# Scores of a local-attention layer: one head per matmul on 64 rows by 32 columns of the array, instead of two heads zero-padded to 128 rows

## The reference, cut to what matters

```python
for i in range(DEPTH):                     # 6
    x = attn_layer(shift_tokens(x), Wqkv[i], q_scale[i], k_scale[i], Wo[i]) + x
    x = ffn_layer(shift_tokens(x), ln_g[i], ln_b[i], W1[i], b1[i], W2[i], b2[i]) + x

# attn_layer
q, k = l2norm(q) * qs, l2norm(k) * ksc     # per head, then rotary with cos, sin, scale
# local_attention: bq has 32 queries of a window, bk2 the 64 keys of this and the window before
sim = jnp.einsum('bhwie,bhwje->bhwij', bq, bk2) * QK_SCALE
sim = jnp.where(mask, -jnp.finfo(sim.dtype).max, sim)
attn = jax.nn.softmax(sim, -1)
out = jnp.einsum('bhwij,bhwje->bhwie', attn, bv2)
```

## Time and profile before

| | us |
|---|---|
| median of 3 runs | 2127.57 (2124.98 to 2128.31) |
| profiled execution, its own time | 2129.41 |
| span of the profiled execution | 2127.6 |
| PE busy | 1861.1 (87%) |
| DVE busy | 1542.8 (73%) |
| ACT busy | 1382.8 (65%) |
| POOL busy | 1261.5 (59%) |
| local layers, first to last scores | 525.3 to 2042.3 |
| mean granted clock of PE | 0.951 |

### The profile page before, as it was taken

One profiled execution on the slowest core, in us unless ns is written; L12 is line 12 of the kernel. 1 busy time (PEld: TensorE's weight loads), 2 busy tenths in 40 slices (PEclk: granted clock), 3 DMA queues, 4 the chain that ended last, 5 costly groups with the idle time before them and its releaser, 6 DMA issues. The chain is left out here.

```text
span 2127.6 us, 47771 instructions
## 1 busy us (share of the span) xinstructions
PE 1861.1 (87%) x18048; PEld 1032.7 (49%) x18048; DVE 1542.8 (73%) x2543; ACT 1382.8 (65%) x2862; POOL 1261.5 (59%) x1111
## 2 busy tenths in 40 slices
PE   3787787865799999999999999999999999999984
PEld 2333333343455555555555555555555555555541
DVE  2667666623687888878788878888878888878753
ACT  1243343432778777778777777877787877787751
POOL 3303030003787777777787777787777787777731
PEclk9698988977899999999999999999999999999996
DMA  7000000022433234233433225333343322323300
GB/s 159 1 2 1 2 1 1 1 60 49 101 77 74 66 81 89 72 75 75 83 80 78 68 67 98 71 80 71 72 85 76 85 66 69 76 66 79 83 21 20
DMA packets 142987, 131.78 MB, mean 62 GB/s; under 512 B 85160, under 2 KB 88808, under 8 KB 142440
## 3 DMA queue, kind: packets, MB, share of 16 engines
q1 hardware_dynamic: 142768, 128.83, 27.1%
HBM read 20.94 MB, written 1.05 MB: 10 GB/s over the span
## 5 line engine op out<-in xcount | busy, mean ns | idle before, releaser
L970 ACT ACTIVATE prob<-s_in,lower,rq 128x64 f32<-128x64 f32 x1536 | 537.9, 430 | 80.6 <-POOL lower L1079 78.5
L831 PE MATMUL bank_a<-x_shift,wqk_sb 128*128 128x512 f32 x768 | 374.6, 611 | 77.0 <-ACT sq L1000 57.9
L850 PE MATMUL bank_y<-zT,wvo 128*128 128x512 f32 x768 | 345.7, 593 | 0.0
L1059 POOL TENSOR_TENSOR sumk<-sq 128x512 f32<-128x512 f32 x96 | 122.5, 1276 | 278.2 <-ACT sq L1000 278.2
L831 PEld LDWEIGHTS bank_a<-x_shift,wqk_sb 128*128 128x128 f32 x768 | 140.1, 193 | 269.5 <-issue 148.2
L850 PEld LDWEIGHTS bank_y<-zT,wvo 128*128 128x128 f32 x768 | 146.1, 190 | 184.2 <-issue 184.2
L863 PEld LDWEIGHTS bank_z<-kpad,qpair 128*32 128x32 f32 x6144 | 164.6, 110 | 101.0 <-issue 98.9
L461 DVE TENSOR_REDUCE a_negmax<-a_max 128x1 f32<-128x512 f32 x256 | 164.6, 684 | 60.7 <-PE a_max L176 60.1
L863 PE MATMUL bank_z<-kpad,qpair 128*32 128x128 f32 x6144 | 187.6, 274 | 23.9 <-ACT zT L966 22.0
L377 ACT ACTIVATE a_prob<-a_sT 128x1024 f32<-128x1024 f32 x128 | 128.8, 1023 | 119.4 <-PE a_sT L208 118.2
L438 POOL TENSOR_TENSOR a_rstd<-a_mv,eps 128x4 f32<-128x4 f32 x4 | 0.8, 200 | 330.1 <-DVE a_mv L517 330.1
(11 more groups left out here) (161 smaller groups left out, 3944.7 us busy)
## 6 DMA issues: line engine op xcount, KB each, us to landing
qpair<-qfin SPq DMA_DIRECT2D x384, 128.0 KB, 2.4
kpad<-kfin SPq DMA_DIRECT2D x768, 64.0 KB, 2.0
wqk_sb<-in_wqkv SPq DMA_DIRECT2D x24, 256.0 KB, 5.6
xk_prev<-xk_own SPq DMA_DIRECT2D x24, 192.0 KB, 2.4
ffn_sb<-in_ffn SPq DMA_DIRECT2D x6, 537.5 KB, 3.9
wv_in<-in_wqkv SPq DMA_DIRECT2D x12, 256.0 KB, 4.9
wo_in<-in_wo SPq DMA_DIRECT2D x6, 512.0 KB, 6.3
xk_prev<-xk_own SPq DMA_DIRECT2D x24, 48.0 KB, 2.3
```

The lines of the kernel that those rows point to most:

```text
L831: last = pe.matmul(bank_a[:, half, :], wqk_sb[:, layer_of(u) % 2, part, half, g * P:(g + 1) * P], cols(u), start=True, stop=True)
L850: last = pe.matmul(bank_y[:].rearrange("p (t w q) -> p t w q", w=WPT, q=WIN), wvo[:, layer_of(u), GH * g + hh, :], zT[:, n % 2, :, :, hh, ...
L970: last = act.activation(prob[:, n % 2, i, :], s_in[:, n % 2, i, :], ACT.Exp, bias=lower[:, n % 2, i:i + 1], scale=rq[:, n % 2, i:i + 1])
L1059: pool.tensor_tensor(sumk[:], sq[:, 0, :], sq[:, 1, :], ALU.add).then_inc(sumk_ok, 1)
```

## The change

Both heads of a pair keep their 64 features together on 64 partitions: the even head on partitions 0 to 63, the odd one on 64 to 127, in `qpair` and in `kpad` alike. `kpad` has no zero copies any more and is half as large. Each scores matmul takes one head: 64 rows, 32 query columns, 64 keys. There are 64 of them a quarter instead of 32, for tile `t`, pair `p`, window `w` and head `e`; the heads `e` write to different banks (`bank_z[:, e]`). The queries need 8 transfers of 32 partitions instead of 4 of 64. The order of the 16 blocks of scores (4 tiles by 4 heads) becomes head parity, tile, pair; the masks, the query norms, the weighted sum's access to `pT` and the choice of `wvo` follow this order.

```diff
-        kpad = sb("kpad", [P, 2, 2, WIN + L])
+        kpad = sb("kpad", [P, 2, WIN + L])
...
-                    for p in range(2):
+                    for hh in range(GH):
+                        p, e = hh // 2, hh % 2
                         for half in range(2):
-                            sp.dma_start(qpair[64 * half:64 * half + 64, p, :],
-                                         qfin[64 * p:64 * p + 64, half, :]).then_inc(qpair_in, 16)
+                            to = 64 * e + 32 * half
+                            sp.dma_start(qpair[to:to + 32, p, :],
+                                         qfin[32 * hh:32 * hh + 32, half, :]).then_inc(qpair_in, 16)
                     after(sp, kfin_ok, n)
                     for hh in range(GH):
                         p, e = hh // 2, hh % 2
                         for half in range(2):
-                            to = 64 * half + 32 * e
-                            sp.dma_start(kpad[to:to + 32, p, e, WIN:WIN + L],
+                            to = 64 * e + 32 * half
+                            sp.dma_start(kpad[to:to + 32, p, WIN:WIN + L],
                                          kfin[32 * hh:32 * hh + 32, half, :]).then_inc(kpad_in, 16)
...
-                                             pT[at, n % 2, c, t * GH:(t + 1) * GH, :].rearrange("p h q -> p (h q)"),
+                                             pT[at, n % 2, c].rearrange("k (e t p) q -> k t e p q", e=2, t=TPB)[:, t],
...
-                                     wvo[:, layer_of(u), GH * g + hh, :],
+                                     wvo[:, layer_of(u), GH * g + 2 * (hh % 2) + hh // 2, :],
...
                 for t in range(TPB):
                     for p in range(2):
                         for w in range(WPT):
-                            at = t * P + w * WIN
-                            c = (t % 2) * 2 * P + p * P
-                            last = pe.matmul(bank_z[WIN * w:WIN * w + WIN, t // 2, c:c + P],
-                                             qpair[:, p, at:at + WIN],
-                                             kpad[:, p, :, at:at + 2 * WIN], start=True, stop=True,
-                                             skip_group_check=True)
+                            for e in range(2):
+                                at, rows = t * P + w * WIN, slice(64 * e, 64 * e + 64)
+                                c = t * P + p * 2 * WIN
+                                last = pe.matmul(bank_z[WIN * w:WIN * w + WIN, e, c:c + 2 * WIN],
+                                                 qpair[rows, p, at:at + WIN], kpad[rows, p, at:at + 2 * WIN],
+                                                 start=True, stop=True, skip_group_check=True)
                 last.then_inc(s_mm, 1)
...
-                    after(pe, qpair_in, c, 64)
+                    after(pe, qpair_in, c, 128)
...
-                        last = pe.matmul(bank_f[:, t * GH:(t + 1) * GH], sumq[:, t * P:(t + 1) * P], pick_head[:],
+                        last = pe.matmul(bank_f[:, 0:TPB * GH].rearrange("q (e t p) -> q t e p", e=2, t=TPB)[:, t], sumq[:, t * P:(t + 1) * P], pick_head[:],
...
-                    after(pool, qpair_in, n - 1, 64)
+                    after(pool, qpair_in, n - 1, 128)
...
-                last = pool.memset(pick_head[32 * hh:32 * hh + 32, hh:hh + 1], 1.0)
+                last = pool.memset(pick_head[32 * hh:32 * hh + 32, 2 * (hh % 2) + hh // 2:2 * (hh % 2) + hh // 2 + 1], 1.0)
...
-                                      mask_sb[:, 4:5, :].broadcast_to([P, 8, 2 * WIN]), ALU.add).then_inc(mask_ok, 1)
+                                      mask_sb[:], ALU.add).then_inc(mask_ok, 1)
...
-            dve.memset(kpad[:].rearrange("p a b n -> p (a b n)"), 0.0).then_inc(kpad_zero, 1)
+            dve.memset(kpad[:].rearrange("p a n -> p (a n)"), 0.0).then_inc(kpad_zero, 1)
...
-    return np.stack([np.where(m, np.float32(0), low) for m in [first] * GH + [ok] * GH], 1).astype(np.float32)
+    return np.stack([np.where(m, np.float32(0), low) for m in [first] * 2 + [ok] * 6], 1).astype(np.float32)
```

## The result

| | before | changed |
|---|---|---|
| median | 2127.18 (2124.98 to 2128.31) | 2164.14 (2159.28 to 2167.26) |
| profiled execution, its own time | 2129.41 | 2167.26 |
| span | 2127.6 | 2165.5 |
| mean granted clock of PE | 0.951 | 0.937 |
| from the 9th block of scores to the 92nd | 1333.0 | 1355.1 |

The ratio is 1.0173, with the 95% interval 1.0152 to 1.0194: slower by 1.7%, clear of the noise, and above the predicted range, which ended at 2150.

What follows compares the result with a forecast made beforehand. PE looked like the bound, though not all of a shorter scores block would be regained: 36 us gained less 10 for clock falls is 26 off the median's 2127.57, forecast 2101 us, with 8 in 10 between 2078 and 2150.

Steps and rivals of the forecast that it cites:

- Instructions come too slowly: Rival: PE waits for instruction packets in some quarters; block 1.4 to 1.8 us, gain only 5 to 20 us; chance 0.07.
- Step (3): Query and key transfers on SP: four more issues cost 0 to 0.3 us in one quarter of four, taken as 0.
- Step (1): Scores matmuls: eight tiles at once, block 1.22 us instead of 1.96, saving 0.74 us a quarter.
- Starts too close: Rival: issue paces the scores block; loses from 0.013 us a start, up to 160 us slower, 2288 us; chance 0.22.
- Step (2): What the shorter block gives back by quarter: 0.39, 0.74, 0.45 and 0, so 1.58 us a unit, 36 us in all.
- Step (4): PE's clock: first-quarter idle grows to 2.22 us; falls in one unit of three at 1.3 us, 10 us, bounds 0 to 30.
- Step (5): Everything else (masks, `pick_head`, `wvo`, access to `pT`, the memset): no further effect, each 0.

Runs made afterwards that it cites:

- e15: Changed kernel with four query transfers (heads 2 and 3 not moved, scores from zeros) and padding waits behind the first three matmuls of L852 only: 2103.85 us.
- e2: Changed kernel with four of its eight query transfers; heads 2 and 3 get no queries, their scores are computed from zeros: 2142.60 us.
- e16: Kernel before, with padding waits behind the first three matmuls of L852 only: 2136.99 us.
- e1: Kernel before, with the queries moved in eight transfers of 32 partitions instead of four of 64, old matmuls kept: 2152.29 us.
- e6: Kernel before, with each scores matmul split into two of 64 keys, so 256 instructions a block, four tiles at once, old transfers: 2165.53 us.
- e14: Changed kernel, whole computation, with the queries' first halves moved early and padding waits behind the first three matmuls of L852 only: 2111.85 us.
- e8: Changed kernel plus padding waits between L852's matmuls, putting the border of two instruction packets in the middle of every scores block: 2147.19 us.
- e10: Changed kernel with four query transfers (heads 2 and 3 not moved, scores from zeros) and padding putting the packet border mid-block: 2123.81 us.
- e11: Changed kernel, whole computation, with the queries' first halves moved early and padding putting the packet border mid-block: 2129.76 us.
- e9: Changed kernel with padding waits placed so that the packet border falls within 8 instructions behind the end of every scores block: 2394.83 us.
- e13: Kernel before, with the same padding waits behind L852's matmuls as the mid-block padded run of the changed kernel: 2143.02 us.
- e3: Changed kernel with half the scores left out from the second quarter on (128 PE instructions a block instead of 256), all transfers kept: 2110.00 us.
- e12: Changed kernel without padding, with SP moving the queries' first halves while POOL computes the second: 2159.71 us.

## Why the prediction was wrong

**The sum had no term for the supply of instructions**, and this is the first failed step; it decided the sign. The rival "Instructions come too slowly" had the right mechanism and the wrong size. I worked out 1.2 us a packet from the queue's share of 16 engines, and a block of 1.4 to 1.8 us in some quarters, still a gain. That share is a mean over time; what counts is how long PE waits from the packet's start, 2.4 us at 1384.11. And the stall does not spread over the block: it comes whole, 1.4 us in the mean and up to 2.5, in one quarter of five, and in six cases of 15 the clock falls behind it. e15 against e2 puts it at 2142.60 - 2103.85 = 39 us, or 49 if the padding costs e15 the 10 that it costs e16, the clock's falls behind the stalls included. I gave it 0.07. With the 21.5 us of the late keys and the 33 that the shorter block gives, 49 + 21.5 - 33 is 37.5, where the change lost 37.0.

**Step (3), "the shorter block covers it. I take 0",** is the second failed step. Its arithmetic of the landing was right to some tenths (a wait of 0 to 0.3 us at the fourth quarter's end), but it took each of the 16 issues at its mean and the keys as late in one quarter only. PE's idle ahead of the scores is above 0.4 us at the end of the fourth quarter in 15 of 21 units, up to 1.4, and at the end of the second, where I had written 1.5 us to spare, in 8 of 21, up to 1.3. Of SP's issues of queries and keys 36 take over 0.75 us between 560 and 2080 us, where 6 did before, and a chain with no slack pays for each. A fall of the clock can follow, as it did behind the wait at 1348.95 (0.90 in that quarter's window). The late keys cost 24 us alone (e1) and 21.5 in the change (against e2).

**Step (1)** took the eight tiles at once for likeliest, and the start of the block bears it out: 29 matmuls start within the first 0.22 us where eight did, and e6's row beside L866's says the same. The size was off: 1.48 us, not 1.22, so 0.48 saved, not 0.74. 128 starts take 1.26 us, 0.0099 apart in the mean of their 127 intervals, where I had 0.007. The first 33 lie within 0.24 us, 0.0076 apart and near what I had; the other 95 come 0.0107 apart. No run tells what holds these up. The rival "Starts too close" named this spacing as its place, but from 0.013 on as the point where it decides, and that was not reached.

**Step (2)** was right in its places: the fourth quarter gave 0, the others the whole 0.48, also the first, where I had capped it at 0.39 by ACT's wait for the Gelu's matmuls. That wait does not cap it, because ACT's work ahead of it moves too: before, `hid` began 5.66 us behind the scores, in the changed kernel 5.18. 1.44 us a unit in place of 1.58, shown in e14's windows (17.57, 15.35, 15.77, 14.22, where the prediction had 17.7, 15.0, 15.8, 14.2).

**Step (4)** foresaw falls of the clock from 2.22 us of idle. In the changed kernel the idle stayed at 1.87, because ACT's chain moved along with PE, and its eight falls are all behind stalls or late keys. In e8, e10 and e11, with 2.00, they came in 14 to 16 of 21 units and at 1.5 us each, where I had one unit in three and 1.3 us.

**Step (5)**: for what it lists (the masks, `pick_head`, `wvo`, the access to `pT`) 0 held, as e15's stretch leaves nothing over. "Nothing else" did not, for want of the term above.

## What to carry to other kernels

Where a change makes more and shorter instructions, count how many fall in one packet of the instruction queue (256 here) and how long the engine takes for them. Here the queue's mean share of 0.6% said nothing, and the place of the border decided: 0 stalls in e8, 83 in e9. Look for it where a whole packet lasts less than some 3.5 us. The 3.5 us are an estimate from e9: 1.1 us from the block's first matmul to the next packet's start, and 2.4 from there to PE's going on. Blocks of 1.5, 2.05 and 2.6 us all stalled. The sign here was an idle named issue in the middle of a run of like instructions, or a few behind it, every 80 us or so, which is nine packets. And the chain of transfers that was to land just in time was late here, 28 times by up to 1.4 us: price such a chain by the spread of its issues, or start its first part earlier, as e14 does.

## What the hardware showed that I had not expected

The same work took 2147.19 or 2394.83 us by a shift of some 120 instructions in the place of the packets' border. Eight tiles of 64 rows by 32 columns took a start every 9.9 ns over 1.26 us. Ahead of the same projection the clock fell behind 2.00 us of PE idle in 14 to 16 of 21 units with the shorter block (e8, e10, e11), in 5 of 21 with the old one (e13), and never behind 1.87; behind waits for the keys, 0.90 to 1.35 us were enough in e3. So no single length of idle separates the cases. What stays open is why the starts slow down behind the first 33 of a block, why the padding still costs 10 us in e16, of which only 3.8 lie in the repeating stretch, and why e12 has more stalls named issue (25.2 us) than the changed kernel.
